# A linear-attention layer on one core: the masked scores and the state in one product of 128 rows

## The chip, the core and the metric

The kernel runs on one core of a Trainium2 chip. The core has five engines that run their own instruction streams and meet at semaphores: TensorE (PE, matrix products into the accumulation memory PSUM), VectorE (DVE), ScalarE (ACT), GpSimd (POOL) and SyncE (SP), which here only issues DMAs. The metric is the time of one execution in microseconds of device time. A single execution was also recorded by the hardware profiler; every row below is from that one.

## What is computed

Eight sequences of 1024 tokens with 512 features go through an attention layer without softmax and through a linear layer, each behind a layer norm and with a residual:

```python
def step(carry, inp):
    kv, ksum = carry
    qt, kt, vt = inp
    kv = kv + kt[..., :, None] * vt[..., None, :]
    ksum = ksum + kt
    num = jnp.einsum('bhi,bhij->bhj', qt, kv)
    den = jnp.einsum('bhi,bhi->bh', qt, ksum)[..., None] + EPS
    return ((kv, ksum), num / den)
...
q, k, v = split(x @ W_attn + b_attn); q, k = elu(q) + 1, elu(k) + 1     # 16 heads of 32
y = lax.scan(step, init, (q, k, v))[1] @ W_proj + b_proj
...
x = x + attn(layernorm(x))
x = x + ffn(layernorm(x))      # ffn: x and the weight rounded to float8, product, + bias
```

(The last lines are put together from the reference's functions.) The kernel does not step token by token: within 64 tokens it forms the scores k·q, masks them and multiplies by v; what came before the 64 tokens is held in a state of 32 x 33 numbers per head (32 columns of kv and one of ksum) that is multiplied by q.

## The kernel before

The 8192 tokens are 64 tiles of 128 (NT), four tiles are one batch of 512 columns for the projection (j, c = divmod(n, 4)), eight tiles are one sequence (PER). In a tile the first 64 tokens are half a = 0, the others a = 1.

Each engine's program is written out by hand, one loop over n with the steps of tile n in a fixed order; nothing is scheduled by a planner. On PE a tile is: `scores(n)`, `from_state(n)`, two chunks of the projection of the next batch (`ahead(chunks(n)[0])`, 12 products of 512 columns each), `k_tokens(n + 1)` (four transposes of k), the third chunk, `values(n)`, `update(n + 1)`, `proj(n - 1)` and `ffn(n - 2)`. A batch has twelve chunks, three per tile: eight of q and k features, four of v. So tiles with c = 0 and c = 1 have three feature chunks, c = 2 has two and a v chunk, c = 3 has three v chunks. I call the three chunks A, B and C. The last five tiles have one chunk or none.

- `scores(n)` makes 32 products of 32 rows x 64 columns: keys x queries of one head and half. They land in the PSUM tensor S, one bank for each of the four heads h of a group g.
- `from_state(n)` makes 16 products q x `mid` (the state after the first half, for a = 1) and 16 q x `state` (for a = 0), started into Y, the upper part of S's banks. In a sequence's first tile the 16 with `state` are left out.
- `values(n)` adds to them, in 32 products of 64 rows x 64 columns, the masked scores `sm` x `v1` (33 columns: 32 of v and a one, which gives the denominator). `valued` crosses the halves of the output, so that four such products fit side by side.
- `update(n)` makes k x v of both halves; DVE adds them up into `mid` and `state`.

A feature chunk goes from PSUM through ACT (exp L441, relu L444) and DVE (L620) into qk; a v chunk through DVE (L628) alone. The masking is split: DVE takes two of four heads (L637), ACT copies the other two out of PSUM (`scores`, into `sm`) and POOL masks them (L891). Behind `values` DVE makes the denominator, its reciprocal and y (L659 to L674), ACT and POOL split y into two halves of 16 bits, SP transposes them by DMA (`yt`), PE projects, DVE adds the result to x (L687, x1) and takes its statistics, POOL normalises (L864, L866: x2), ACT rounds x2 to float8 and copies it to bf16 (`t2`: x28, x2b), SP transposes that (`x2t`), PE makes the FFN, ACT copies it (o) and DVE adds it to x (L697).

Every engine works its instructions off in order. ACT's order in a tile was: copy of the scores, chunk A, `ln1_parts` (the upper half of xn), chunk B, `k_tokens` (ktok), `t2(n - 2)`, chunk C, yhl, o. PE's PSUM targets other than S are four banks taken in turn; a bank is free when the engine that reads it is through.

## Time and profile before

| | us |
|---|---|
| median of 3 runs | 1022.61 (1021.32 to 1024.68) |
| profiled execution, device time | 1024.16 |
| its span, first to last instruction | 1022.4 |
| PE busy | 984.3 (96%) |
| DVE busy | 687.4 (67%) |
| POOL busy | 537.7 (53%) |
| ACT busy | 457.7 (45%) |

A row of a timeline gives the start of a group of equal instructions in microseconds, how long the group lasted, engine and line, the operation, output <- input by the program's names, shapes and count. For PE the name before the comma is the moving operand and the one behind it the stationary one, whose loading is a record of its own under PEld; a product in f32 has two records of each kind. The x1 of a tile is DVE's L687, x2 POOL's L866.

### The profile page before, as it was taken

To read this page: it belongs to the slowest core of one execution; us is meant where nothing else is said; L and a number is where in the kernel's file an instruction comes from. 1 tells how busy PE (TensorE), PEld (TensorE's weight loads), DVE (VectorE), ACT (ScalarE), POOL (GpSimd) and SP (SyncE) were. 2 spreads that over 40 slices of the span, in tenths; PEclk is the share of its full clock that TensorE was granted. 3 is DMA by queue.
4 is the path that set the end of the run, shared out by engine and by line. 5 is a ranking of instruction groups with operands and counts; after the bars stand their busy time and mean duration, and the time that the engine had idled before them with its cause. 6 is when DMAs were issued, how large, how long until landed. Compare 5 with 4: busy or idle time off the path is not lost.

```text
span 1022.4 us, 43585 instructions
## 1 busy us (share of the span) xinstructions
PE 984.3 (96%) x19504; PEld 547.6 (54%) x19504; DVE 687.4 (67%) x1447; ACT 457.7 (45%) x715; POOL 537.7 (53%) x524
## 2 busy tenths in 40 slices
PE   5999999999999999999999999999999999999896
PEld 2455555555555555555555555555555555555463
DVE  6887667676667667666666666676666767655475
ACT  5653453534535354452544534354452643534322
POOL 3565575564564564564565564564464564453233
PEclk9989999999999999999999999999999999999999
DMA  8714334333434323333533345334333344322111
GB/s 271 110 34 100 70 73 85 75 80 82 77 80 88 82 70 90 80 70 88 77 82 86 75 70 91 79 70 92 71 76 94 67 83 91 64 60 54 34 57 52
DMA packets 185355, 82.51 MB, mean 81 GB/s; under 512 B 165840, under 2 KB 165840, under 8 KB 185168
## 3 DMA queue, kind: packets, MB, share of 16 engines
q1 hardware_dynamic: 185168, 79.73, 36.4%
q8 instruction: 153, 2.51, 1.0%
q14 instruction: 34, 0.28, 0.1%
HBM read 22.81 MB, written 16.78 MB: 39 GB/s over the span
## 4 chain that ended last, share of the span: by engine, by line
PE 80%; DMA 6%; DVE 4%; issue 4%; ACT 2%; SPq 1%; POOL 1%; ACTq 0%; POOLq 0%
PE R L227 64%; PE S L227 14%; DMA x2t<-x2b 6%; PE R L231 2%; DVE xnhl L614 2%; SPq L968 1%; ACT rel L444 1%; DVE raw L791 0%; DVE st L597 0%; DVE xs L687 0%; POOL st L864 0%; DVE qk L620 0%; ACT x L432 0%; DMA xs<-in_L_attn_x 0%; ACT x2b L432 0%
## 5 line engine op out<-in xcount | busy, mean ns | idle before, releaser
L227 PE MATMUL R<-xt,wh 128*128 128x512 f16 x1024 | 307.6, 383 | 2.4 <-ACT wh L432 2.4
L898 POOL TENSOR_TENSOR yhl<-y,yhl 128x512 f16<-128x512 f32 x60 | 71.4, 1190 | 328.8 <-ACT yhl L432 328.8
L620 DVE SCALAR_TENSOR_TENSOR qk<-qk,rel 128x512 f32<-128x512 f32 x128 | 124.5, 975 | 166.9 <-ACT rel L444 166.2
L227 PE MATMUL R<-xt,wl 128*128 128x512 f16 x512 | 194.4, 381 | 0.0
L227 PE MATMUL R<-wh,xt 128*128 128x512 f16 x512 | 160.3, 379 | 0.0
L864 POOL TENSOR_TENSOR st<-st,half 128x1 f32<-128x1 f32 x128 | 91.1, 711 | 129.4 <-DVE st L602 117.4
L227 PEld LDWEIGHTS R<-xt,wh 128*128 128x128 f16 x1024 | 97.1, 98 | 110.2 <-issue 4.4
L441 ACT ACTIVATE qk<-R,bqk,wm 128x512 f32<-128x512 f32 x128 | 99.5, 777 | 117.9 <-PE R L227 117.9
L227 PE MATMUL R<-wph,yt 128*128 128x512 f16 x512 | 132.9, 382 | 1.2 <-DVE yt L680 1.2
L432 ACT ACTIVATE yhl<-y 128x512 f16<-128x512 f32 x60 | 37.8, 630 | 171.9 <-DVE y L674 171.9
L886 POOL TENSOR_TENSOR xs<-xs,bp 128x512 f32<-128x512 f32 x64 | 108.8, 1705 | 0.0
L444 ACT ACTIVATE rel<-R,bqk,wm 128x512 f32<-128x512 f32 x128 | 98.4, 769 | 2.3 <-DVE qk L620 2.3
L614 DVE TENSOR_TENSOR xnhl<-xn,xnhl 128x512 f16<-128x512 f32 x56 | 85.1, 1520 | 18.0 <-ACT xnhl L432 17.9
L227 PE MATMUL R<-wl,xt 128*128 128x512 f16 x256 | 97.0, 379 | 0.0
L597 DVE BATCH_NORM_STATS2 st<-xs 128x6 f32<-128x512 f32 x128 | 88.4, 691 | 6.3 <-DMA xs<-in_L_attn_x 3.9
L628 DVE SCALAR_TENSOR_TENSOR v<-R,wm,bv 128x512 f32<-128x512 f32 x64 | 47.8, 748 | 57.9 <-PE R L227 57.8
L907 POOL TENSOR_TENSOR xs<-xs,bf 128x512 f32<-128x512 f32 x64 | 81.5, 1273 | 5.3
L227 PEld LDWEIGHTS R<-xt,wl 128*128 128x128 f16 x512 | 50.3, 98 | 61.3 <-issue 1.5
L432 ACT ACTIVATE o<-R 128x512 f16<-128x512 f32 x64 | 38.2, 597 | 100.0 <-PE R L227 100.0
L227 PEld LDWEIGHTS S<-v,sm 64*64 64x64 f32 x4096 | 65.8, 134 | 28.6 <-issue 26.7
L227 PEld LDWEIGHTS R<-wh,xt 128*128 128x128 f16 x512 | 50.0, 98 | 55.6
L891 POOL TENSOR_TENSOR sm<-sm,causal 128x512 f32<-128x512 f32 x60 | 78.9, 1315 | 0.0
(91 smaller groups left out, 1500.3 us busy)
## 6 DMA issues: line engine op xcount, KB each, us to landing
xs<-in_L_attn_x SPq DMA_DIRECT2D x64, 256.0 KB, 3.4
out<-xs SPq DMA_DIRECT2D x64, 256.0 KB, 2.6
raw<-in_L_attn_W_attn SPq DMA_DIRECT2D x3, 1024.0 KB, 9.4
xs<-in_L_attn_W_proj SPq DMA_DIRECT2D x4, 256.0 KB
raw<-in_L_ffn_weight SPq DMA_DIRECT2D x1, 1024.0 KB, 16.5
x2t<-x2b SPq DMA_TRANSPOSE x62, 3.6
xt<-xnhl SPq DMA_TRANSPOSE x60, 3.1
yt<-yhl SPq DMA_TRANSPOSE x60, 3.4
```

The source lines that it names most:

```text
L227: return e.matmul(out, a, b, start=start, stop=stop, skip_group_check=True)
L432: return e.activation(out, in_, ACT.Copy, **more)
L441: e.activation(dst[:, i, :], bank["qkv", j, i][:, :], ACT.Exp, scale=UN[i // 4], bias=bqk[:, i:i + 1])
L444: e.activation(rel[:, u % 2, :], bank["qkv", j, i][:, :], ACT.Relu, scale=UN[i // 4], bias=bqk[:, i:i + 1]).then_inc(s_relu, 1)
L597: e.bn_stats(row[:, 0:6], src).then_inc(s_bn, 1)
L614: e.tensor_tensor(xnhl[:, m % 4, 1, :], xn[:, m % 2, :], xnhl[:, m % 4, 0, :], ALU.subtract).then_inc(s_xlo, 1)
L620: e.scalar_tensor_tensor(qk[j % 2][:, i, :], qk[j % 2][:, i, :], 1.0, rel[:, (u - 1) % 2, :], ALU.min, ALU.add).then_inc(s_phi, 1)
L864: e.tensor_tensor(row[:, 10:11], row[:, 9:10], half[:, :], ALU.pow).then_inc(s_rs, 1)
L886: e.tensor_tensor(x, x, bp[:, :], ALU.add).then_inc(s_xb, 1)
L891: e.tensor_tensor(sm[:, 2:4, :, :], sm[:, 2:4, :, :], causal_over(2), ALU.mult).then_inc(s_sel, 1)
L898: e.tensor_tensor(yhl[:, n % 2, 1, :], y[:, :], yhl[:, n % 2, 0, :], ALU.subtract).then_inc(s_yl, 1)
L907: e.tensor_tensor(x, x, bf[:, :], ALU.add).then_inc(s_x1b, 1)
```

## The change

The state products are no longer products of their own. `sm`, which now lies in a part of `raw`, has for each half a all 128 partitions: on one half of them the masked scores (64 tokens), on the other the queries of two or four heads (32 features per head, two heads in 64 partitions). `v1` has 128 partitions per half as well: v of the 64 tokens on one half of them, and on the other the state of the head that is meant, with zeros where the other head of the pair stands. One product of 128 rows then gives masked scores x v plus q x state, and `values` has 32 of them, all started and ended by themselves.

- PE: `from_state` is gone. `values` has 32 products of 128 rows x 64 columns with 33 moving columns.
- ACT: the copy of scores is gone. `queries(n)` copies q into `sm` in four operations (64 partitions, 512 elements), `spread(n)` copies `state` and `mid` into `v1` in eight (32 partitions, 132 elements). `t2(n - 2)` stands at the head of the tile, ahead of `queries`.
- DVE: masks all heads in two operations of 64 partitions and 1024 elements; writes v in two of 64 partitions; makes y in one; no longer makes the lower half of xn (L614). `state` is zeroed at a sequence's start, so every tile has both states.
- POOL: no longer masks; makes the lower half of xn; at the start it clears `v1` (five slots of 1056 elements) and sets its ones.
- SP: x2t's transpose is issued ahead of xt's and of the FFN weight's.
- In tile 0 chunk C comes behind `values` and `update`, and the rounding of the FFN weight stands later.

```diff
-            def from_state(n):
...
+            def values(n):
                 src, v, j, c = parts(n)
+                pe.wait_ge(s_smd, n + 1)
+                pe.wait_ge(s_q, n + 1)
+                pe.wait_ge(s_v, n + 1)
+                pe.wait_ge(s_spread, n + 1)
                 for g in range(4):
+                    for h in range(4):
+                        for a in range(2):
+                            mm = matmul(Y[half_rows(a), h, g * W:(g + 1) * W], sm[:, h, a, g * HALF:(g + 1) * HALF],
+                                        v[:, a, 4 * g + h, :], True, True)
                 mm.then_inc(s_av, 1)
```

```diff
+            def queries(n):
...
+                if n:
+                    act.wait_ge(s_av, n)
+                for a in range(2):
+                    for p in range(2):
+                        q = src[half_rows(p), 0:4, tokens(n, a)[0]].unsqueeze(1).broadcast_to([HALF, 2, 4, HALF])
+                        dst = sm[half_rows(1 - a), 2 * p:2 * p + 2, a, :].rearrange("p h (g t) -> p h g t", g=4)
+                        made = copy(dst, q)
+                made.then_inc(s_q, 1)
+
+            def spread(n):
...
+                for a in range(2):
+                    act.wait_ge(*((s_mid, n + 1) if a else (s_state, n + 1)))
+                    held = mid if a else state[:, n % 2, :]
+                    for h in range(4):
+                        at, rows = HALF * (1 - a) + 32 * (h % 2), slice(32 * h, 32 * h + 32)
+                        made = copy(v[at:at + 32, a, :, h, :], held[rows, :].rearrange("p (g w) -> p g w", g=4))
+                made.then_inc(s_spread, 1)
...
+                    if n >= 2:
+                        t2(n - 2)
+                    if n:
+                        queries(n)
                     ahead(chunks(n)[0][:1])
+                    if n:
+                        spread(n)
```

```diff
             def scores(n):
-                for i, h in enumerate((0, 2) if tail(n) else (0,)):
...
-                    e.tensor_tensor(sm[:, h:h + 2, :, :], scored(h), causal_over(2), ALU.mult).then_inc(s_smd, 1)
+                dve.wait_ge(s_score, n + 1)
...
+                for a in range(2):
+                    dst = sm[half_rows(a), :, a, :].rearrange("p h (g t) -> p h g t", g=4)
+                    made = e.tensor_tensor(dst, scored(a), causal_over(a), ALU.mult)
+                made.then_inc(s_smd, 1)
...
             for n in range(NT + 2):
                 if 1 <= n <= NT:
                     t_y(n - 1)
+                if n >= 2:
+                    t2(n - 2)
+                if n + 8 < NT:
+                    t1(n + 8)
```

ACT, in a tile with three feature chunks (c = 0), before, the whole tile but its last row, the copy o. `qk` and `rel` are a chunk's exp and relu, `x` and `x2b` the two copies of x2:

```order
L432 ACTIVATE sm<-S 128x512
L441 ACTIVATE qk<-R,bqk,wm 128x512
L444 ACTIVATE rel<-R,bqk,wm 128x512
L432 ACTIVATE xnhl<-xn 128x512
L441 ACTIVATE qk<-R,bqk,wm 128x512
L444 ACTIVATE rel<-R,bqk,wm 128x512
L432 ACTIVATE ktok<-R 128x512
L432 ACTIVATE x<-x 128x512
L432 ACTIVATE x2b<-x 128x512
L441 ACTIVATE qk<-R,bqk,wm 128x512
L444 ACTIVATE rel<-R,bqk,wm 128x512
L432 ACTIVATE yhl<-y 128x512
```

The same engine and tile now, up to ktok; chunk C, yhl and o follow. `raw<-qk` are the query copies, `v<-state` and `v<-mid` the state copies:

```order
L407 ACTIVATE x<-x 128x512
L407 ACTIVATE x2b<-x 128x512
L407 ACTIVATE raw<-qk 64x2x256 x4
L416 ACTIVATE qk<-R,bqk,wm 128x512
L419 ACTIVATE rel<-R,bqk,wm 128x512
L407 ACTIVATE v<-state 32x4x33 x4
L407 ACTIVATE v<-mid 32x4x33 x4
L407 ACTIVATE xnhl<-xn 128x512
L416 ACTIVATE qk<-R,bqk,wm 128x512
L419 ACTIVATE rel<-R,bqk,wm 128x512
L407 ACTIVATE ktok<-R 128x512
```

The two copies of x2 moved from behind ktok to the front, and twelve new copies stand ahead of xnhl, chunk B and ktok.

PE, from one tile's values to the next one's score and state products, before:

```order
L227 MATMUL S<-v,sm 64x33 x32
L227 MATMUL R<-v,ktok 32x33 x32
L227 MATMUL R<-wph,yt 128x512 x4
L227 MATMUL R<-wpl,yt 128x512 x4
L227 MATMUL R<-wph,yt 128x512 x4
L227 MATMUL R<-wft,x2t 128x512 x4
L227 MATMUL S<-qk 64x64 x32
L227 MATMUL S<-state,qk 64x33 x4
L227 MATMUL S<-mid,qk 64x33 x4
```

and now, with the first product of the next chunk as the last row:

```order
L219 MATMUL S<-v,raw 64x33 x32
L219 MATMUL R<-v,ktok 32x33 x32
L219 MATMUL R<-wph,yt 128x512 x4
L219 MATMUL R<-wpl,yt 128x512 x4
L219 MATMUL R<-wph,yt 128x512 x4
L219 MATMUL R<-wft,x2t 128x512 x4
L219 MATMUL S<-qk 64x64 x32
L219 MATMUL R<-xt,wh 128x512 x2
```

The last two rows of before came four times in turn; they are gone, and the values read `raw` (the place of `sm`) instead of `sm`.

DVE, from the mask to x1 in a tile with c = 0, before:

```order
L637 TENSOR_TENSOR sm<-S,causal 128x512
L620 SCALAR_TENSOR_TENSOR qk<-qk,rel 128x512
L614 TENSOR_TENSOR xnhl<-xn,xnhl 128x512
L620 SCALAR_TENSOR_TENSOR qk<-qk,rel 128x512 x2
L659 TENSOR_SCALAR den<-S 128x16
L661 RECIPROCAL den<-den 128x16
L669 TENSOR_TENSOR y<-S,den 128x2x128
L674 TENSOR_TENSOR y<-S,den 64x2x128 x2
L648 TENSOR_TENSOR mid<-R,state 128x132
L651 TENSOR_TENSOR state<-R,mid 128x132
L687 SCALAR_TENSOR_TENSOR xs<-R,wm,xs 128x512
```

and now:

```order
L640 TENSOR_TENSOR raw<-S,causal 64x4x256 x2
L617 SCALAR_TENSOR_TENSOR qk<-qk,rel 128x512 x3
L665 TENSOR_SCALAR den<-S 128x16
L667 RECIPROCAL den<-den 128x16
L675 TENSOR_TENSOR y<-S,den 128x512
L651 TENSOR_TENSOR mid<-R,state 128x132
L654 TENSOR_TENSOR state<-R,mid 128x132
L686 SCALAR_TENSOR_TENSOR xs<-R,wm,xs 128x512
```

All three chunks' last steps still stand ahead of den, y and x1; xnhl is gone from this engine.

## Rows read from the trace of the kernel before

**Rows 1.** The page: busy microseconds, share of the span, instructions of each engine.

```profile
PE 984.3 (96%) x19504; PEld 547.6 (54%) x19504; DVE 687.4 (67%) x1447; ACT 457.7 (45%) x715; POOL 537.7 (53%) x524
```

**Rows 2.** PE's waits: for whom, microseconds in total, times, longest.

```profile
PE R L227 <- DMA x2t<-x2b: 5.9, 13, 0.7
```

**Rows 3.** Timeline of PE, tiles 22 to 24: start, length, instructions.

```profile
401.07 0.46 PE L227 MATMUL R<-v,ktok 64*32 64x33 f32 x32
401.46 1.04 PE L227 MATMUL R<-wph,yt 128*128 128x512 f16 x4
...
405.02 0.85 PE L227 MATMUL S<-qk 32*64 32x64 f32 x60
...
405.72 0.22 PE L227 MATMUL S<-qk 32*64 32x64 f32 x1
...
406.50 0.39 PE L227 MATMUL R<-wh,xt 128*128 128x512 f16 x1
...
414.81 1.14 PE L227 MATMUL S<-v,sm 64*64 64x33 f32 x64
415.87 0.76 PE L227 MATMUL R<-v,ktok 64*32 64x33 f32 x64
416.56 1.04 PE L227 MATMUL R<-wph,yt 128*128 128x512 f16 x4
...
420.12 0.86 PE L227 MATMUL S<-qk 32*64 32x64 f32 x61
```

**Rows 4.** PE's weight loads: by form (mean ns last), then by tile (min/median/max).

```profile
L227 PEld LDWEIGHTS S<-v,sm 64*64 64x64 f32 x4096 | 65.8, 134 | 28.6 <-issue 26.7 <-DVE sm L637 1.9
...
L227 PEld LDWEIGHTS R<-ident,wm x8: 190/190/333, 12.8 to 49.9; 128*128 128x128 f32 x8
```

**Rows 5.** Timeline of ACT, tile 24 (c = 0).

```profile
428.16 0.59 ACT L432 ACTIVATE ktok<-R 128x512 f32<-128x512 f32 x1
428.64 0.63 ACT L432 ACTIVATE x<-x 128x512 fp8e4<-128x512 f32 x1
429.30 0.63 ACT L432 ACTIVATE x2b<-x 128x512 bf16<-128x512 fp8e4 x1
429.85 0.78 ACT L441 ACTIVATE qk<-R,bqk,wm 128x512 f32<-128x512 f32 x1
430.53 0.77 ACT L444 ACTIVATE rel<-R,bqk,wm 128x512 f32<-128x512 f32 x1
```

**Rows 6.** ACT's instructions by form: a copy of 2048 elements.

```profile
L432 ACT ACTIVATE raw<-raw 128x2048 fp8e4<-128x2048 f32 x1 | 1.9, 1902 | 0.0
```

**Rows 7.** Timeline of DVE, tiles 22 to 24.

```profile
404.26 0.75 DVE L687 SCALAR_TENSOR_TENSOR xs<-R,wm,xs 128x512 f32<-128x512 f32 x1 [0.93 <-PE R L227]
...
407.80 0.68 DVE L637 TENSOR_TENSOR sm<-S,causal 128x512 f32<-128x512 f32 x1
...
431.33 0.69 DVE L620 SCALAR_TENSOR_TENSOR qk<-qk,rel 128x512 f32<-128x512 f32 x1 [1.52 <-ACT rel L444]
...
432.43 0.42 DVE L669 TENSOR_TENSOR y<-S,den 128x256 f32<-128x256 f32 x1
432.87 0.86 DVE L674 TENSOR_TENSOR y<-S,den 64x256 f32<-64x256 f32 x2
...
434.30 0.75 DVE L687 SCALAR_TENSOR_TENSOR xs<-R,wm,xs 128x512 f32<-128x512 f32 x1
```

**Rows 8.** Timeline of POOL: x2 of the tile whose x1 is above.

```profile
407.32 0.77 POOL L866 TENSOR_SCALAR x<-xs,st 128x512 f32<-128x512 f32 x1
```

**Rows 9.** Timeline of PE: first score products of tiles 1, 59, 60 and 63.

```profile
64.76 0.89 PE L227 MATMUL S<-qk 32*64 32x64 f32 x35 [2.40 <-DVE y L674]
...
955.77 0.50 PE L227 MATMUL S<-qk 32*64 32x64 f32 x33
...
970.60 0.66 PE L227 MATMUL S<-qk 32*64 32x64 f32 x37
...
999.45 0.70 PE L227 MATMUL S<-qk 32*64 32x64 f32 x40
```

More of the change, by code:

```diff
@@ L27 @@
 NR = 4
+NV = 5
 ORDER = (0, 4, 1, 5, 2, 6, 3, 7, 8, 9, 10, 11)
@@ L340, in values @@
+                mm.then_inc(s_score, 1)
             def values(n):
                 src, v, j, c = parts(n)
-                first = n % PER == 0
-                pe.wait_ge(s_smd, masked_dve(n))
-                if not tail(n):
-                    pe.wait_ge(s_sel, n + 1)
+                pe.wait_ge(s_smd, n + 1)
+                pe.wait_ge(s_q, n + 1)
                 pe.wait_ge(s_v, n + 1)
-                pe.wait_ge(s_one, 2)
-                for h in (0, 2):
-                    for g in range(4):
-                        for a, i in ((0, h), (1, h), (0, h + 1), (1, h + 1)):
-                            rows = tokens(n, a)[1]
-                            mm = matmul(Y[valued(a, i), i, g * W:(g + 1) * W], sm[rows, i, g, :],
-                                        v[rows, c, 4 * g + i, :], first and a == 0 and g == 0, True)
+                pe.wait_ge(s_spread, n + 1)
@@ L414, in _ @@
                         k_tokens(n + 1)
-                    ahead(chunks(n)[1])
+                    if n:
+                        ahead(chunks(n)[1])
                     values(n)
@@ L418, in _ @@
                         update(n + 1)
+                    if n == 0:
+                        ahead(chunks(n)[1])
                 if 1 <= n <= NT:
@@ L484, in k_tokens @@
                 copy(ktok[:, n % 2, :], bank["ktok", n][:, :]).then_inc(s_ktok, 1)
-            def scores(n):
-                if not tail(n):
-                    act.wait_ge(s_score, 4 * n + 4)
-                    if n:
-                        act.wait_ge(s_av, n)
-                    copy(sm[:, 2:4, :, :], scored(2)).then_inc(s_scopy, 1)
+            def queries(n):
+                src, v, j, c = parts(n)
+                for g in range(4):
+                    act.wait_ge(s_phi, phi_count(j, g))
+                act.wait_ge(s_wl, 6)
+                if n:
[7 more added lines that the diff above has]
+            def spread(n):
+                v = v1[:, n % NV, :, :, :].rearrange("p a (g h) w -> p a g h w", g=4)
+                act.wait_ge(s_one, 2)
+                if n >= NV:
+                    act.wait_ge(s_av, n - NV + 1)
+                for a in range(2):
[5 more added lines that the diff above has]
+                made.then_inc(s_spread, 1)
             def t2(n):
@@ L562, in _ @@
             phi(0, 7)
+            queries(0)
+            k_tokens(0)
             proj_size()
-            k_tokens(0)
             ffn_half()
@@ new lines, in v_out @@
+                dve.wait_ge(s_one, 2)
+                if n >= NV:
+                    dve.wait_ge(s_av, n - NV + 1)
+                for a in range(2):
+                    rows = half_rows(a)
+                    made = e.scalar_tensor_tensor(v1[rows, n % NV, a, :, 0:32], heads(bank["qkv", j, 8 + t][rows, :]),
+                                                  UN_V[rows], heads(bv[rows, :]), ALU.mult, ALU.add)
+                made.then_inc(s_v, 1)
+            def scores(n):
+                dve.wait_ge(s_score, n + 1)
+                dve.wait_ge(s_causal, 3)
+                if n:
+                    dve.wait_ge(s_av, n)
+                for a in range(2):
+                    dst = sm[half_rows(a), :, a, :].rearrange("p h (g t) -> p h g t", g=4)
+                    made = e.tensor_tensor(dst, scored(a), causal_over(a), ALU.mult)
+                made.then_inc(s_smd, 1)
@@ L844, in _ @@
                         t_y(n - 1)
-                    ahead(chunks(n)[1])
+                    if n:
+                        ahead(chunks(n)[1])
                     values(n)
@@ L849, in _ @@
                     if n == 0:
+                        ahead(chunks(n)[1])
                         proj_weight()
                         ffn_round()
+                    if n == 1:
+                        ffn_sum()
                 if 1 <= n <= NT:
@@ L886, in add_bp @@
                 e.tensor_tensor(x, x, bp[:, :], ALU.add).then_inc(s_xb, 1)
-            def scores(n):
-                if not tail(n):
-                    pool.wait_ge(s_scopy, n + 1)
-                    e.tensor_tensor(sm[:, 2:4, :, :], sm[:, 2:4, :, :], causal_over(2), ALU.mult).then_inc(s_sel, 1)
             def values(n):
@@ L913, in _ @@
             e.memset(half[:, :], -0.5).then_inc(s_half, 1)
-            for i in range(2):
-                e.memset(v1[i][:, :, :, 32:33], 1.0).then_inc(s_one, 1)
             for m in range(4):
@@ L926, in _ @@
             pool.wait_ge(s_causal, 3)
+            e.memset(v1[:, :, :, :, :], 0.0).then_inc(s_blank, 1)
+            pool.wait_ge(s_blank, 1)
+            for a, base, step in ((0, -HALF, 1), (1, HALF - 1, -1)):
+                ones = v1[:, :, a, :, 32:33].rearrange("p i h w -> p (i w) h")
+                e.affine_select(out=ones, in_=ones, compare_op=ALU.is_ge, fill=1.0, base=base,
+                                pattern=[[0, NV], [0, 16]], channel_multiplier=step).then_inc(s_one, 1)
             ln1(4)
```

121 lines of the change are left out of this document (40 added, 81 removed).

## The prediction

> **What bounds the kernel now.** I read the page's engine shares first, then PE's waits, then one tile's timeline engine by engine. PE is busy 96% of the span; no other engine is above 67% [rows 1]. PE's waits inside the loop are small: the largest that comes back is the one for x2t, 5.9 us in 13 places [rows 2]. So the time is the sum of PE's pieces, and these repeat. From tile 23's first score product to tile 24's is 405.02 to 420.12, 15.10 us: scores and state products 1.48 (405.02 to 406.50), three projection chunks with the k transposes 8.31 (to 414.81), values 1.06 (to 415.87), update 0.69 (to 416.56), output projection and FFN 3.56 (to 420.12) [rows 3]. The 58 full tiles 1 to 58 take 64.76 to 955.77, 891.0 us, 15.36 each; tiles 60 to 62, without chunks or with one, take 970.60 to 999.45, 28.85 us [rows 9].
>
> The other engines matter through one loop, so I note where its steps lie against a score start S. DVE's x1 (L687) starts at S - 0.76 (404.26 against 405.02) [rows 3, 7]. POOL's x2 ends at 407.32 + 0.77 = 408.09, which is S + 3.07 [rows 8]. Before, ACT copies x2 only at about S + 8.5 (428.64 against 420.12) and nobody waits long for that.
>
> **PE: what goes and what comes.** The state products go. In tile 23 the last score product starts at 405.72, 0.70 after the first; with the 0.14 that lie between the last values product (near 415.73, see below) and the update at 415.87, scores alone should last 0.84 instead of 1.48 [rows 3]. That is 0.64 less. Tiles that open a sequence (8 of 64) have half of these products; without them 56 x 0.64 = 36 us would go from PE.
>
> The values keep 32 products (64 records), but each now takes 128 rows x 64 columns, so that only two fit side by side (the column halves) where four 64 x 64 ones did. The 64 records before take 1.06 us; the last starts near 415.73 (414.81 + 1.14 - 0.22), so a step of four records takes about 0.92 / 15 = 0.06 us [rows 3]. What sets that step: a weight load of 64 columns lasts 134 ns, a load of 128 rows x 128 columns in f32 190 ns, 0.875 ns per column, so 64 columns are 0.056 us [rows 4]. The second load has 128 rows and lies on the same line, so I take it that the rows cost nothing and the columns set the step. Then 64 records in steps of two are 32 x 0.06 = 1.92, with the turnover 2.0 us: +0.94 per tile, 60 us in all. The bounds: if the step is not the load's, each record might cost what it does now, 1.06 (+0); if the two column halves do not overlap, 64 x 0.06 = 3.8 us (+2.8). I take +0.94, because the step fits the load. PE's own tile is then 15.10 - 0.64 + 0.94 = 15.4 us.
>
> On the overlap a rule can be weighed. From 401.07 to 401.46 stand 32 records of an update that reads rows 0 to 63 alone, in four column groups: 12 ns each, less than the 28 ns that 32 columns of weights take at 0.875 ns [rows 3, 4]. So loads do overlap between column groups of the same rows. The Trainium skill, "TensorE: Matmul & The Clock Gate", section "The mechanism", says that a weight load overlaps products in flight only when its row group differs; this row speaks against it. By that rule the values would take the 3.8 us, and it is a rival below.
>
> **ACT: the copies, and where they stand.** One copy of half of the heads' scores goes. Four query copies (64 partitions, 512 elements) and eight small ones of the state (32 partitions, 132 elements) come. In a row of copies ACT's next starts 0.48 after ktok (428.16 to 428.64) and 0.55 after x2b (429.30 to 429.85) [rows 5]; I take 0.53 for 512 elements. From 512 to 2048 elements a copy grows from 0.63 to 1.90 us, 0.83 ns an element [rows 5, 6], so 132 elements come at 0.53 - 0.31 = 0.22. Queries 4 x 0.53 = 2.12, state 8 x 0.22 = 1.76. No small ACT copy is in the trace: by bytes alone it would be 0.14 (state 1.1), at the price of a full copy 0.53 (4.2). I take 0.22, which keeps the fixed part of the rows, and use 0.35 as a likely upper end.
>
> ACT's work grows by 3.3 us in a tile of 15, of which it was busy 45% [rows 1], so there is room, but not where the copies are put. Its order in a tile is now: x2's two copies, queries, chunk A's exp and relu, state copies, xnhl, chunk B, ktok, chunk C, yhl, o. The first of these waits for x2 at S + 3.07, and everything stands behind it. PE wants the values at S + 0.84 + 8.31 = S + 9.15. ACT: 3.07 + 1.19 (x 0.66, x2b 0.53) + 2.12 + 1.36 (two of 0.68) + 1.76 + 0.1 = S + 9.6. That alone would cost 0.4. The rest is later still: xnhl 0.53, chunk B 1.36, ktok 0.60 end at S + 12.0, where PE (values over at 9.6 + 2.0 = 11.6) wants to update; and chunk C's relu ends at S + 13.3, behind which DVE, in order, does C's last step before it turns to y and x1.
>
> **The loop that closes.** From x1 of one tile to x1 of the next where all three chunks are features (c = 0 and 1): x1 to x2's end 3.83 [rows 7, 8]; x2's copies 1.19, queries 2.12, A 1.36, state 1.76, xnhl 0.53, B 1.36, ktok 0.53, C's exp 0.68 and relu 0.77, 0.03 [rows 5, 6]; DVE from C to y 1.10 (431.33 to 432.43), y as one operation of 512 elements 0.75 (as x1), then 0.57 through mid and state to x1 (y's end 433.73 to 434.30) [rows 7]. Sum 16.6. Where C is a v chunk (c = 2) it ends at ktok: 3.83 + 1.19 + 2.12 + 1.36 + 1.76 + 0.53 + 1.36 + 0.60 = 12.75, update 0.69, projection to x1 2.80 (401.46 to 404.26): 16.2. With no feature chunk (c = 3) it is 14.5, and PE's 15.4 decides. Of tiles 1 to 58 these are 29, 15 and 14: 481 + 244 + 216 = 940 us, +49 over 891.
>
> In the last tiles PE has 10 us of work and the loop without chunks is 3.83 + 1.19 + 2.12 + 1.86 + values 2.0 + 0.69 + 2.80 = 14.5: three of them 43.2 against 28.85, +14.3. In the last one values start at S + 8.3 instead of about 3, +5.6 with the longer product and without state products. Together +20.
>
> **What is free or nearly so.** DVE masks in two operations of 64 partitions and 1024 elements (under 2 x 1.36, twice the 0.68 of L637) from about S + 2.8 (407.80 against 405.02): over by 5.6, before 9.15 [rows 7]. v in two halves +0.75 per v, y in one -0.5, xnhl's subtraction goes to POOL where the mask of 1.3 went away: both have gaps. On SP x2's transpose now stands ahead of xt's; x2b is there at S + 4.4, xt's input later than before (behind xnhl), still some 3 us before a batch's first chunk needs it. x2t's 5.9 us of waits go, and are in my sum, which has none. POOL's clearing of v1 at the start delays layer norms that ACT and DVE reach late anyway; ACT's two microseconds for tile 0's queries lie beside PE's last chunks: 0, between -2 and +5.
>
> **Sum.** Profiled execution 1024.2 (span 1022.4, 1.8 outside it, 1.6 above the median 1022.6): 1024.2 + 49 + 20 = 1093.
>
> **Rivals.**
> 1. *PE stays the bound*: ACT's copies cost less and hide. Needed: queries and state together 2.7 instead of 3.9 us in c = 0 and 1. Then 58 x 15.4 = 894 (+3), tail +20: 1047. For it: ACT is 45% busy. Against: ten steps of the loop are measured rows. 10%.
> 2. *Faster*: the wide product costs per record what the small one did (1.06) and the copies hide too. PE's tile 14.5, 58 of them 839 (-52), tail +18: 990. It turns from slower to faster where the average tile falls under 15.0. For it: half the state work gone is real; against: the load's price per column, and that the loop does not hold a values step in c = 0 to 2 at all, so a cheap product alone saves only c = 3 and the tail (some 17 us). 5%.
> 3. *The state copies are dear* (0.35 or more): +1.04 in 44 tiles and the tail: 1143 and above. 12%.
> 4. *The column halves run one after the other*: PE's tile 17.3, 58 of them 1002 (+111), tail +27: 1162. By the rule above; the 12 ns row speaks against. 4%.
>
> My forecast with cheap to middling state copies (0.14 to 0.33: 1061 to 1135) has 67%; 2% are left for about no change. The range 1045 to 1135 takes in rival 1. Faster or slower by 0.3%, some 3 us, is about what a measurement of this kernel tells from no change: faster 5%, same 2%, slower 93%.
>
> **What would show it.** Right: PE's busy time falls or stays while its waits grow; new waits of PE for ACT's v copies before values and for ktok before update; values' 64 records in 2.0 us; tiles of 16.6, 16.6, 16.2 and 15.4 in turn; ACT waits for x2 at each tile's head; ACT's 132-element copies 0.2 apart; x2t no longer waited for. Wrong: values in 1.1 us (rival 2's half), tiles all of 15.4 (rival 1), DVE reaching x1 before PE has the projection in c = 0 and 1.

## Result and the profile after

The changed kernel takes 1200.82 us (median of 4 runs, 1196.81 to 1204.99) against 1023.64 (1021.32 to 1025.77) for the kernel before, run beside it: ratio 1.173, 95% interval 1.168 to 1.178. The sign was as forecast, the size was not: 1093 was forecast, 1135 was the upper end. The profiled execution lasts 1200.12 us, its span 1198.4; the span of before was 1022.4.

The page of the changed kernel: busy time of each engine, the granted clock in 40 slices, and the chain of work that ended last, as shares of the span (columns as in [rows 1]).

```profile
PE 1037.6 (87%) x15664; PEld 595.8 (50%) x15664; DVE 697.0 (58%) x1395; ACT 745.3 (62%) x1423; POOL 509.7 (43%) x521
...
PEclk9998999999999999999999999999999999998977
...
ACT 40%; PE 25%; DVE 14%; issue 11%; POOL 9%; DMA 0%; DVEq 0%
```

PE falls from 96% to 87%, and the chain is no longer PE's: ACT holds 40% of it, and DVE and POOL take part. It is a loop over engines, as forecast. The waits (columns as in [rows 2]) name its two joints:

```profile
ACT x L407 <- POOL x L866: 154.6, 62, 6.6
...
PE S L219 <- ACT v L407: 129.9, 62, 8.2
...
PE R L219 <- ACT ktok L407: 9.3, 22, 0.4
```

ACT waits 62 times for x2, 2.5 us each, and PE 62 times for ACT's state copies. The wait for x2t of [rows 2] is gone. By groups of instructions (busy us, mean ns of one | idle before them):

```profile
L219 PE MATMUL S<-v,raw 128*64 128x33 f32 x4096 | 154.5, 239 | 130.2 <-ACT v L407 129.9
```

One tile of ACT, tile 25 (c = 1, PE's first score product at 492.88), from the last tile's o to this tile's chunk C, answers to [rows 5]:

```profile
492.98 0.60 ACT L407 ACTIVATE o<-R 128x512 f16<-128x512 f32 x1 [1.34 <-PE R L219]
495.98 0.63 ACT L407 ACTIVATE x<-x 128x512 fp8e4<-128x512 f32 x1 [2.40 <-POOL x L866]
496.64 0.63 ACT L407 ACTIVATE x2b<-x 128x512 bf16<-128x512 fp8e4 x1
497.30 2.55 ACT L407 ACTIVATE raw<-qk 64x512 f32<-64x512 f32 x4
499.87 0.78 ACT L416 ACTIVATE qk<-R,bqk,wm 128x512 f32<-128x512 f32 x1
500.55 0.77 ACT L419 ACTIVATE rel<-R,bqk,wm 128x512 f32<-128x512 f32 x1
501.35 1.28 ACT L407 ACTIVATE v<-state 32x132 f32<-32x132 f32 x4
502.64 1.29 ACT L407 ACTIVATE v<-mid 32x132 f32<-32x132 f32 x4
503.96 0.63 ACT L407 ACTIVATE xnhl<-xn 128x512 f16<-128x512 f32 x1
...
506.96 0.79 ACT L419 ACTIVATE rel<-R,bqk,wm 128x512 f32<-128x512 f32 x1
```

POOL makes the x2 that ACT waits for:

```profile
495.18 0.77 POOL L866 TENSOR_SCALAR x<-xs,st 128x512 f32<-128x512 f32 x1
```

ACT stands idle from 493.6 to 496.0 for x2, with the queries behind it that need nothing of x2. From there it runs without a gap to chunk C's relu (507.75), and only then can DVE go on. DVE's x1 of this tile and of the next, and what stands ahead of the second (this answers to [rows 7]):

```profile
492.12 0.75 DVE L686 SCALAR_TENSOR_TENSOR xs<-R,wm,xs 128x512 f32<-128x512 f32 x1 [0.61 <-PE R L219]
...
507.78 0.69 DVE L617 SCALAR_TENSOR_TENSOR qk<-qk,rel 128x512 f32<-128x512 f32 x1 [1.14 <-ACT rel L419]
...
510.14 0.74 DVE L686 SCALAR_TENSOR_TENSOR xs<-R,wm,xs 128x512 f32<-128x512 f32 x1
```

x1 to x1 is 18.02 us (492.12 to 510.14): POOL's x2 ends at 495.95, 3.83 after x1 as forecast, ACT's unbroken run takes to 507.75, DVE the rest. PE's values in tiles 24 and 25, and the score product that opens tile 25 (answers to [rows 3]):

```profile
485.36 3.07 PE L219 MATMUL S<-v,raw 128*64 128x33 f32 x64 [1.98 <-ACT v L407]
...
492.88 0.91 PE L219 MATMUL S<-qk 32*64 32x64 f32 x64
...
504.08 2.06 PE L219 MATMUL S<-v,raw 128*64 128x33 f32 x64 [1.98 <-ACT v L407]
```

Both tiles wait 1.98 us for the state copies. In tile 25 the values take 2.06, in tile 24 the same 64 records take 3.07, at a lower clock. By stretches (length, busy PE, PEld, DVE, ACT, POOL with counts, granted clock, DMA share, GB/s): tiles 24, 25, 27 (c = 3) and 59:

```profile
474.16:492.88 18.72, 16.74 (x250) 9.90 (x249) 9.48 (x20) 12.75 (x24) 7.84 (x8) 0.91 0.27 65
492.88:510.79 17.91, 15.51 (x249) 8.81 (x248) 9.30 (x20) 12.75 (x24) 7.04 (x9) 1.00 0.30 68
...
529.73:545.69 15.96, 15.46 (x249) 8.79 (x248) 11.91 (x24) 8.62 (x18) 7.85 (x8) 1.00 0.32 76
...
1094.19:1111.66 17.47, 11.80 (x225) 7.99 (x224) 7.91 (x15) 8.09 (x17) 4.63 (x5) 0.80 0.17 40
```

So tiles last 17.9 (c = 0, 1, 2) and 16.0 (c = 3), some 18.7 to 18.9 with a stretch at the lower clock (1.2 instead of 2.4 GHz). Tiles 1 to 58 take 65.03 to 1094.19, 1029.2 us; what follows takes 104.2, before 66.6 [rows 9].

The experiments below are quoted with what was expected of each. A ratio is to the kernel before, run beside it on the same chip (its median 1021.72, 1019.5 and 1023.23 in the three larger groups of runs and 1024.45 beside the last kernel). "Head" is the place at which ACT's order of a tile begins.

### The profile page after: what moved, and what is told of

Read it like the earlier page. It is cut to its first block, busy times and chain, and to the rows that moved or that the text cites. A ratio compares the mean times of both kernels' runs of the same rounds, so it can differ in the third digit from the quotient of the medians.

```text
span 1198.4 us, 36528 instructions
## 1 busy us (share of the span) xinstructions
PE 1037.6 (87%) x15664; PEld 595.8 (50%) x15664; DVE 697.0 (58%) x1395; ACT 745.3 (62%) x1423; POOL 509.7 (43%) x521
## 4 chain that ended last, share of the span: by engine, by line
ACT 40%; PE 25%; DVE 14%; issue 11%; POOL 9%; DMA 0%; DVEq 0%
PE R L219 16%; ACT raw L407 13%; ACT v L407 10%; PE S L219 9%; ACT qk L416 5%; POOL st L864 5%; ACT rel L419 5%; POOL x L866 4%; DVE xs L686 4%; DVE st L601 4%; ACT x L407 3%; ACT x2b L407 2%; DVE st L603 1%; ACT ktok L407 1%; DVE st L606 1%
## 5 line engine op out<-in xcount | busy, mean ns | idle before, releaser
L617 DVE SCALAR_TENSOR_TENSOR qk<-qk,rel 128x512 f32<-128x512 f32 x128 | 97.3, 762 | 341.8 <-ACT rel L419 341.6
L219 PE MATMUL S<-v,raw 128*64 128x33 f32 x4096 | 154.5, 239 | 130.2 <-ACT v L407 129.9
L219 PEld LDWEIGHTS S<-v,raw 128*64 128x64 f32 x4096 | 148.6, 157 | 158.4 <-issue 157.6
L881 POOL TENSOR_TENSOR xnhl<-xn,xnhl 128x512 f16<-128x512 f32 x60 | 72.4, 1207 | 230.1 <-ACT xnhl L407 230.1
L407 ACT ACTIVATE raw<-qk 64x512 f32<-64x512 f32 x256 | 160.9, 628 | 3.8
L640 DVE TENSOR_TENSOR raw<-S,causal 64x1024 f32<-64x1024 f32 x128 | 155.7, 1217 | 0.9
L219 PE MATMUL R<-wph,yt 128*128 128x512 f16 x512 | 141.6, 402 | 1.4 <-DVE yt L679 1.4
L407 ACT ACTIVATE x<-x 128x512 fp8e4<-128x512 f32 x62 | 39.1, 630 | 154.6 <-POOL x L866 154.6
L629 DVE SCALAR_TENSOR_TENSOR v<-R,wm,bv 64x512 f32<-64x512 f32 x128 | 96.0, 750 | 16.4 <-PE R L219 13.9
L888 POOL TENSOR_TENSOR xs<-xs,bp 128x512 f32<-128x512 f32 x64 | 82.4, 1288 | 4.7
```

Of the source, the lines that this page charges most:

```text
L219: return e.matmul(out, a, b, start=start, stop=stop, skip_group_check=True)
L407: return e.activation(out, in_, ACT.Copy, **more)
L617: e.scalar_tensor_tensor(qk[j % 2][:, i, :], qk[j % 2][:, i, :], 1.0, rel[:, (u - 1) % 2, :], ALU.min, ALU.add).then_inc(s_phi, 1)
L629: made = e.scalar_tensor_tensor(v1[rows, n % NV, a, :, 0:32], heads(bank["qkv", j, 8 + t][rows, :]), UN_V[rows], heads(bv[rows, :]), ALU.m ...
L640: made = e.tensor_tensor(dst, scored(a), causal_over(a), ALU.mult)
L881: e.tensor_tensor(xnhl[:, m % 4, 1, :], xn[:, m % 2, :], xnhl[:, m % 4, 0, :], ALU.subtract).then_inc(s_xlo, 1)
```

## Experiment 1: the product without its copies

```diff
             def queries(n):
...
+                if n:
+                    return
...
             def spread(n):
...
+                if n >= NV:
+                    return
```

PE's waits for these copies, and DVE's, are lifted as well. The kernel so leaves the state's part out of y from tile 5 on.

> The changed kernel without its query copies after tile 0 and without its state copies after tile 4, so the state's part of y is left out from then on; the wide products and all else stay. Theory A (the loop through ACT's twelve copies behind x2 carries the loss): PE is the bound again with tiles of 15.4 us, 58 of them 894, and the last tiles near the kernel before: 1035 to 1055. Theory B (the wide product and the changed work of PE carry it): little changes, 1150 or more. Theory C (half of it each, the copies and the place of x2's copies): 1080 to 1120.

Measured: 1034.10 us (1033.37 to 1035.59), ratio 1.012 (1.011 to 1.014). PE, one values product between the scores of two tiles:

```profile
483.67 0.91 PE L219 MATMUL S<-qk 32*64 32x64 f32 x64
492.82 2.06 PE L219 MATMUL S<-v,raw 128*64 128x33 f32 x64
499.06 0.91 PE L219 MATMUL S<-qk 32*64 32x64 f32 x64
```

Tiles of 15.39 (483.67 to 499.06) without a wait. So PE's own tile is the 15.4 that was forecast, and the product costs what was worked out; what is left up to 1201, some 167 us, comes in with the copies.

## Experiment 2: x2's copies back behind ktok, and the head alone in the kernel before

In the changed kernel:

```diff
-                    if n >= 2:
-                        t2(n - 2)
                     if n:
                         queries(n)
...
                         k_tokens(n + 1)
+                    if n >= 2:
+                        t2(n - 2)
```

> The changed kernel with x2's two copies back behind ktok on ACT, all copies kept. Theory A1 (it is the wait for x2 at the head, with the copies queued behind it, not ACT's amount of work, 12.8 us of 17.9 busy in a tile): queries start at S + 0.7 instead of S + 4.4, values find their copies, tiles of 15.4 to 15.8: 1040 to 1070, and the clock stays at full. Theory A2 (twelve copies are too much for ACT wherever they stand): above 1120.

Measured: 1051.31 us (1046.74 to 1052.63), ratio 1.028 (1.026 to 1.030): 149 us under the changed kernel, with every copy still there. Most tiles are 15.39; PE waits 10.8 us in 14 places for x2t again.

In the kernel before, the opposite edit, with the transposes' order on SP:

```diff
                 if n < NT:
+                    if n >= 2:
+                        t2(n - 2)
                     scores(n)
...
-                if 2 <= n < NT:
-                    t2(n - 2)
...
+                if n >= 2:
+                    t2(n - 2)
                 if n + 8 < NT:
                     t1(n + 8)
-                if n >= 2:
-                    t2(n - 2)
```

> The kernel before with x2's two copies at the tile's head on ACT and x2t's transpose ahead of xt's on SP, nothing else of the change. Theory: ACT waits for x2 as in the changed kernel, but only the copy of the scores (0.6 us) and no twelve copies stand between it and chunk A; the loop is 3.83 + 1.2 + 0.6 + 1.4 + 0.5 + 1.4 + 0.5 + 1.45 and 3 on DVE = 13.9, under PE's 15.1. The 13 waits for x2t and the stretched tiles (some 10 us in all) go: 1010 to 1020. Rival: the place at the head costs by itself: above 1035.

Measured: 1014.00 us (1013.17 to 1016.22), ratio 0.993 (0.991 to 0.994), below both kernels. ACT at a tile's head, and the chain:

```profile
416.50 0.63 ACT L432 ACTIVATE x<-x 128x512 fp8e4<-128x512 f32 x1 [2.40 <-POOL x L866]
```

```profile
PE 93%; DVE 2%; POOL 1%; issue 1%; ACT 1%; DMA 0%; ACTq 0%; POOLq 0%
```

ACT waits for x2 exactly as long as in the changed kernel (2.40), and here it costs nothing, since the loop behind it is short. No x2t wait is left, and tiles 1 to 58 take 874.6 us instead of 891.0, nearly all 15.1 or less. The place of x2's copies is therefore harmless alone, and so nearly are the other copies alone (experiment 2, first part): it is the two together that cost some 150 us.

A third place, t2 behind chunk A and the layer norm's part, with SP's order as in b_x2_head:

> The kernel before with x2's two copies behind the first chunk and xnhl on ACT, where x2 has long been made, and x2t's transpose ahead of xt's on SP. If the gain of the version with the copies at the head comes from x2t landing before PE asks for it, this one is the same: tiles of 15.10, 1010 to 1018. If it were from the place at the head itself: like the kernel before, 1018 to 1024.

Measured: 1014.58 us (1010.69 to 1016.57), ratio 0.991 (0.988 to 0.995), the same as at the head. The gain of b_x2_head is x2t landing in time, not the head. How much of it is SP's order and how much the earlier copies was not taken apart; in a_x2_back SP's new order alone left PE 10.8 us of waits for x2t.

## Experiment 3: two lines swapped

```diff
-                    if n >= 2:
-                        t2(n - 2)
                     if n:
                         queries(n)
+                    if n >= 2:
+                        t2(n - 2)
```

> The changed kernel with two lines of ACT's tile swapped: the four query copies ahead of x2's two copies. No work is added or left out. Theory A (the loop from x1 through POOL's x2 and ACT): 2.6 us leave the loop, since the queries then run while x2 is still being made; 17.9 - 2.6 = 15.3, so PE's 15.4 decides in nearly every tile, and the last tiles shorten as well: 1030 to 1055. Rival (ACT's whole row of work decides, 12.8 us busy and its waits): above 1120.

Measured: 1052.46 us (1050.19 to 1052.76), ratio 1.028 (1.025 to 1.031). Same instructions, 148 us less. ACT at the head:

```profile
470.07 2.55 ACT L407 ACTIVATE raw<-qk 64x512 f32<-64x512 f32 x4
472.64 0.63 ACT L407 ACTIVATE x<-x 128x512 fp8e4<-128x512 f32 x1
```

The queries fill the time in which x2 is on its way, and ACT then waits for x2 4.3 us in the whole run (154.6 in the changed kernel). The tiles come back to PE's 15.4: with the 2.6 us of queries out of it the loop is under that, and PE sets the pace. That gives 2.5 us in each of 42 tiles and 0.6 in each of the 14 with c = 3, some 114 us; the rest comes in tile 2 (20.1 instead of 23.5), behind tile 58 (88.8 us instead of 104.2) and from the clock, which rises to 0.988 from 0.953. PE's waits for v fall to 24.1 us in 6 places.

## Experiment 4: fewer copies in the loop

The four copies of mid left out:

```diff
-                for a in range(2):
+                for a in range(2 if n < NV else 1):
```

> The changed kernel without the four copies of the state after the first half (mid) from tile 5 on, which leaves that part out of y. A dose of the suspected cost: 1.3 us out of ACT's row. Theory A: every tile with c = 0 to 2 gets 1.3 us shorter plus the clock's share (0.8 in a third of them), c = 3 0.57, the last tiles 1.3 to 2.5 each: 60 to 90 us faster than the changed kernel, 1110 to 1140. If the copies are only partly on the path: under 40 us.

Measured: 1119.27 us (1117.66 to 1120.03), ratio 1.097 (1.094 to 1.101). Most tiles are 16.61 to 16.71 for c = 0 to 2 and 15.39 for c = 3. PE's score products of two tiles in turn, 16.62 apart:

```profile
448.52 0.91 PE L219 MATMUL S<-qk 32*64 32x64 f32 x64
...
465.14 0.91 PE L219 MATMUL S<-qk 32*64 32x64 f32 x64
```

The four copies took 1.29 us (502.64, above), and the tiles gave 1.2 to 1.3 (17.92 - 16.71, 17.92 - 16.61): what stands in ACT's run counts one for one, or nearly. That is the loop, shown by its slope.

## Experiment 5: what the clock took

The lower clock follows PE's waits, so this kernel shortens them without touching the loop: six products of chunk C are made twice, ahead of it.

```diff
+                for a, b in mms[:again]:
+                    matmul(out[:, :], a, b, True, True)
...
-                        ahead(chunks(n)[1])
+                        ahead(chunks(n)[1], 6 if c < 3 and n > 1 else 0)
```

> The changed kernel with six redundant products (1.3 us) ahead of chunk C in tiles with c = 0 to 2, so that PE is busy in a part of the time in which it waits for the state copies; the result is the same. Theory (17 of the stretches at half clock inside the loop make values and the first projection products 0.8 to 1.0 us longer in their tile, and follow from PE's 2 us waits): these go, the clock rises from 0.953, 10 to 18 us faster than the changed kernel, 1183 to 1191. Rival (the clock is hidden in the waits): no change, or slower by up to 44 x 0.3.

Measured: 1184.42 us (1184.03 to 1185.5), ratio 1.160 (1.158 to 1.161): with 1.3 us more of work in 43 tiles it is 16 us faster than the changed kernel. A tile as a stretch:

```profile
467.19:485.11 17.92, 16.77 (x255) 9.41 (x255) 9.30 (x20) 12.75 (x24) 7.05 (x8) 1.00 0.29 68
```

PE's wait for the state copies is down from 1.98 to some 0.5 to 0.7 us a tile. The tile is the loop's 17.92 again, and in the steady tiles the granted clock stays at the higher level (2.4 GHz); over the run it is 0.983 instead of 0.953. So some 16 us of the loss are stretches at 1.2 GHz, and they followed waits of 2 us of an engine that was otherwise busy.

## Experiment 6: what a copy costs on ACT

The copies in a row were forecast 0.53 (512 elements) and 0.22 (132) apart and came 0.64 and 0.325 apart. Series of copies that nobody waits for, behind the last tile of the kernel before, tell why. First, all of them beginning at partition 0:

```diff
+            for i in range(4):
+                copy(raw[:, 0, i, :], y[:, :])
+            for i in range(4):
+                copy(raw[0:HALF, 2, i, :], y[0:HALF, :])
+            for i in range(4):
+                copy(qk[0][:, 4 + i, 0:4 * W], y[:, 0:4 * W])
+            for i in range(4):
+                copy(qk[0][0:32, 4 + i, 256:256 + 4 * W], y[0:32, 0:4 * W])
...
```

> The kernel before with eight series of four independent ACT copies behind its last instruction, each series of another form: how far apart do they start? 128 x 512 and 64 x 512 from SBUF, 128 x 132 and 32 x 132 from SBUF, 128 x 512 and 64 x 512 from PSUM, 128 x 512 with the queries' pattern. Theory P (a copy from SBUF behind one from SBUF never starts before the other's end; the 0.1 us of overlap in the rows of before all have PSUM on one side): 128 x 512 from SBUF 0.64 apart, from PSUM 0.5. Theory Q (copies of fewer than 128 partitions don't overlap): 128 x 512 0.53 apart, 64 x 512 0.64.

Measured (one execution, 1028.29 us), four plus four copies of 512 elements, then four plus four of 132 (a row names the shape of its first copy: the second four of each have 64 and 32 partitions), and four with the queries' pattern:

```profile
1014.56 4.25 ACT L432 ACTIVATE raw<-y 128x512 f32<-128x512 f32 x8
1018.72 1.71 ACT L432 ACTIVATE qk<-y 128x132 f32<-128x132 f32 x8
...
1024.16 2.17 ACT L432 ACTIVATE xt<-qk 128x512 f32<-128x512 f32 x4
```

Eight in 4.16 us (1014.56 to 1018.72), 0.52 apart, with 128 partitions and with 64 alike; eight small ones in 1.62, 0.20 apart, with 32 partitions as with 128; the queries' pattern four in 2.17, the last one 0.63 long, 0.51 apart. Both theories fell, for neither the number of partitions nor the queries' pattern costs anything. What was left is where a copy's partitions lie against those of the one ahead:

```diff
+            for i in range(4):
+                copy(raw[up, 0, i, :], y[low, :])
...
+            for i in range(4):
+                at = up if i % 2 else low
+                copy(raw[at, 2, i, :], y[at, :])
+            for i in range(4):
+                copy(qk[0][32:64, i, 0:4 * W], y[0:32, 0:4 * W])
+            for i in range(4):
+                copy(qk[0][0:32, i, 0:4 * W], y[32 * i:32 * i + 32, 0:4 * W])
+            for i in range(4):
+                copy(qk[0][32 * i:32 * i + 32, 4, 0:4 * W], y[0:32, 0:4 * W])
...
```

> The kernel before with eight series of four ACT copies behind its last instruction. In the series before, copies with all partitions from 0 on started 0.52 (512 elements) and 0.20 (132) apart; in the changed kernel they started 0.64 and 0.325 apart. Theory S (a copy waits for the end of the one before when the set of partitions changes between them): only the series that alternate the half or the quarter of source or target are 0.64 or 0.32 apart. Theory T (when source and target lie on different partitions): the series with a constant shift are slow as well. Theory U (targets with gaps in them): only the last two series, with the patterns of the queries and of the state, are slow.

Measured (one execution, 1032.02 us), each row a stretch of the series: from the lower to the upper half each time; alternating halves (two of them); 32 partitions, from the first to the second group of 32 each time; alternating sources (with the last copy of the series ahead); all three kinds in order of time:

```profile
1016.60 2.19 ACT L432 ACTIVATE raw<-y 64x512 f32<-64x512 f32 x4
...
1020.99 1.27 ACT L432 ACTIVATE raw<-y 64x512 f32<-64x512 f32 x2
...
1023.54 0.92 ACT L432 ACTIVATE qk<-y 32x132 f32<-32x132 f32 x4
1024.17 1.59 ACT L432 ACTIVATE qk<-y 32x132 f32<-32x132 f32 x5
```

Four in 2.19, the last one 0.63 long, are 0.52 apart; two in 1.27 are 0.64 apart; four in 0.92, the last 0.31 long, 0.20; five in 1.59, 0.32. Whether source or target moves makes no difference, and a constant shift between them costs nothing. So in these series ACT's next copy starts some 0.11 us before the end of the one ahead only when it reads and writes the same partitions as that one. (That it does is not enough for every pair: x2b, which reads what x has just written, starts 0.03 us after x's end, 496.64 against 496.61.) The queries read alternating halves, and the state copies go to and from changing groups of 32: every one of them starts after the end of the one before. The Trainium skill, "ScalarE: Activation LUTs", section "What ACT_TABLE_LOAD costs", says that ACTIVATEs in a row overlap by about 93 ns; the rows with a constant place come near it (0.11), those with a changing place show no overlap, and here the measurement decides.

## Experiment 7: the state copies on DVE

```diff
-                        made = copy(v[at:at + 32, a, :, h, :], held[rows, :].rearrange("p (g w) -> p g w", g=4))
+                        made = e.tensor_copy(v[at:at + 32, a, :, h, :], held[rows, :].rearrange("p (g w) -> p g w", g=4))
...
                     scores(n)
+                    spread(n)
```

ACT's own `spread` and its two calls are gone.

> The changed kernel with the eight state copies on DVE, behind the mask, instead of on ACT; x2's copies stay at the head. Theory A: 2.6 us leave the loop of ACT; DVE makes them in some 2 us from S + 5.3, before values at S + 9.15. Loop of c = 0 and 1: 17.9 - 2.6 = 15.3, PE's 15.4 decides: 1040 to 1065 with the last tiles. Rival (ACT's loop is held by the x2 wait and the queries alone): above 1100.

Measured: 1082.45 us (1080.27 to 1084.8), ratio 1.062 (1.058 to 1.065). Tiles of 15.39 for c = 0 to 2, as the shorter run on ACT wants, but 17.07 for c = 3, so the 1040 to 1065 that was expected was missed by 17 us. In tile 27 (c = 3) PE waits 0.56 us for DVE's state copies and 0.99 for the DVE that has a v chunk's bank to empty behind them: the work moved to a second engine that others wait for. With x2's copies behind ktok besides (both edits together):

> The changed kernel with the state copies on DVE and x2's copies back behind ktok. If PE is the bound in every tile, this is its floor: 58 x 15.4 = 894 and last tiles like before, 1025 to 1045: the wide product's price of +0.3 us per tile is left, so it is not faster than the kernel before. Rival: faster than before (under 1018), if PE's steps get shorter when nobody waits.

Measured: 1103.31 us (1101.07 to 1105.16), ratio 1.082 (1.079 to 1.085). This missed as well (1025 to 1045 was expected): the two cures together are worse than either. Most tiles are 15.92, and 16.97 for c = 3. DVE's state copies as a group (mean 773 ns), then DVE's copies in one tile, then POOL in the same stretch:

```profile
L637 DVE COPY v<-state 32x132 f32<-32x132 f32 x256 | 197.9, 773 | 4.6
```

```profile
493.05 0.63 DVE L637 COPY v<-state 32x132 f32<-32x132 f32 x1
493.70 1.35 DVE L637 COPY v<-state 32x132 f32<-32x132 f32 x1
495.06 1.10 DVE L637 COPY v<-state 32x132 f32<-32x132 f32 x1
...
496.41 0.92 DVE L637 COPY v<-mid 32x132 f32<-32x132 f32 x4
```

```profile
492.83 0.77 POOL L864 TENSOR_SCALAR xn<-xs,st 128x512 f32<-128x512 f32 x1
493.69 1.27 POOL L886 TENSOR_TENSOR xs<-xs,bp 128x512 f32<-128x512 f32 x1
494.92 1.15 POOL L879 TENSOR_TENSOR xnhl<-xn,xnhl 128x512 f16<-128x512 f32 x1
```

The first three state copies end at 493.68, 495.05 and 496.16, each 0.08 or 0.09 after the end of a POOL operation (493.60, 494.96, 496.07); the four of mid, with POOL idle, take 0.92 together. In a_spread_dve, where DVE's copies stand otherwise against POOL's work, the eight cost less: state 568 ns and mid 281 in the mean, against 773 and 223. To tell a block from mere lateness, one more kernel writes the same copies as another kind of DVE operation:

```diff
-                        made = e.tensor_copy(v[at:at + 32, a, :, h, :], held[rows, :].rearrange("p (g w) -> p g w", g=4))
+                        src = held[rows, :].rearrange("p (g w) -> p g w", g=4)
+                        made = e.tensor_reduce(v[at:at + 32, a, :, h, :], src.unsqueeze(3), AX.X, ALU.add)
```

> a_both with one thing changed: the eight state copies on DVE are written as reductions over a last axis of one element, the same numbers to the same places. In a_both a copy takes 0.22 us when POOL is idle, and when one meets a POOL operation it ends 0.09 us after that operation (ends 493.68, 495.05, 496.16 against POOL's 493.60, 494.96, 496.07); the state copies last 773 ns in the mean. Theory L (lock): DVE's copy and POOL's operations exclude each other, and a DVE operation of another kind does not. Then a reduction takes 0.2 to 0.3 us whatever POOL does, the tiles come to PE's 15.4 in all four positions, and the time falls from 1103 by 44 x 0.5 + 14 x 1.6 + some 5 in the last tiles to about 1055 (1045 to 1065). The Trainium skill, SBUF - State Buffer, section Who interferes with whom, states this exclusion for DVE copies and excepts the reduction. Theory D (DVE is merely late: the copies wait for something else, or POOL's traffic slows any DVE operation on these rows): the reductions last 0.6 us and more beside POOL as well, tiles stay 15.9 and 17.0, 1095 to 1110.

Measured: 1047.27 us (1045.83 to 1047.94), ratio 1.021 (1.017 to 1.025), 56 us under a_both. DVE's state copies as a group, then four of them in one tile, then the POOL operation beside them:

```profile
L638 DVE TENSOR_REDUCE v<-state 32x132 f32<-32x132 f32 x256 | 72.5, 283 | 4.7
```

```profile
490.67 1.17 DVE L638 TENSOR_REDUCE v<-state 32x132 f32<-32x132 f32 x4
```

```profile
491.31 1.27 POOL L887 TENSOR_TENSOR xs<-xs,bp 128x512 f32<-128x512 f32 x1
```

The reductions take 0.28 us beside POOL's operation (state 283 ns in the mean, mid 280), a little more than a free copy (0.22), and tiles are 15.39 again. So the copies were blocked by POOL's operations. This is what the Trainium skill, "SBUF — State Buffer", section "Who interferes with whom", says: a DVE copy can run in a mode that uses two port pairs, the second of which is shared with GpSimd, whoever issues first holds it for the whole instruction, and a reduction never takes part. The trace agrees, copy by copy, for DVE behind POOL; that POOL waits for a DVE copy is not shown by these rows.

## Why the direction was right and the size wrong

What held, by the prediction's own steps:

- *PE's pieces.* Values 2.06 us as recorded, 1.99 from their start to the update's in a_no_copies (2.0 forecast), scores 0.84 (0.84), PE's tile 15.39 (15.4). The step by columns of weights came out, and with it that the two column halves overlap: rivals 2 and 4 fell on one row, `S<-v,raw` at 504.08. Over b_x2_head, where nothing waits either, the change without its copies costs 1034.1 - 1014.0 = 20 us.
- *The loop and its joints.* ACT waits for x2 at the head, PE for v, now and then for ktok; in tile 25 DVE reaches x1 with the projection done (tile 24, whose values ran at the lower clock, has DVE wait 0.61 for it at 492.12); x1 to x2's end 3.83 to the digit. Rival 1 (PE stays the bound) fell on PE's 129.9 us of waits.
- *What was held to be free.* The mask on DVE, the subtraction on POOL and SP's order cost nothing in steady tiles, and x2t's waits went: a_no_copies has all of this and tiles of 15.39.

**The step that failed** is the price of a copy in the ACT part: "I take 0.53 for 512 elements", from the rows ktok to x and x2b to qk [rows 5], and from it 0.22 for 132. Those rows keep the same 128 partitions, and the copies to be priced do not (experiment 6). Measured in tile 25 against the forecast: x and x2b to the first query 1.32 instead of 1.19, queries 2.57 instead of 2.12, relu to the first state copy 0.80 instead of 0.68, state 2.61 instead of 1.76. That is 1.55 a loop, and by experiment 4 what is added there counts one for one or nearly. Added to the forecast's 16.6 and 16.2 it gives 18.1 and 17.8, where the tiles are 17.92; with no chunk in it, the loop of 14.5 becomes 15.9, where c = 3 has 15.96. Rival 3 looked at the right place, but its state copies of 0.35 or more did not come (0.325 apart), and its 1.04 us a tile left out the queries. The range ended at 1135 because it gave a margin to the state copies alone: none to the queries, the clock, the opening or the last tiles.

The miss of 107 us (1200.1 - 1093) adds up as follows. Tiles 1 to 58 took 1029.2 instead of 940, 89 more:

- 56 of them, tiles 3 to 58, at the loop's 17.92 (42 tiles) and 15.96 (14 tiles) are 976.1; the forecast had 28 x 16.6 + 14 x 16.2 + 14 x 15.4 = 907.2. **The copies' price: 69 us.** In it are 8 us of c = 3, where the forecast let PE decide and the loop of 15.96 is 0.57 above PE's 15.39.
- Measured, the 56 took 990.6 (103.63 to 1094.19): **14 us more, the clock.** The forecast had no term for it. Experiment 5 gives 16 for the whole kernel.
- **Tile 2, 23.5 instead of 16.2: 7 us,** less 1.5 that tile 1 came under. This was not foreseen either. DVE and PE of the changed kernel there:

```profile
80.50 3.45 DVE L790 TENSOR_TENSOR raw<-raw 128x512 bf16<-128x512 fp8e4 x4
83.88 0.74 DVE L686 SCALAR_TENSOR_TENSOR xs<-R,wm,xs 128x512 f32<-128x512 f32 x1
...
95.43 3.63 PE L219 MATMUL S<-v,raw 128*64 128x33 f32 x64 [6.10 <-ACT v L407]
```

The reordered opening puts a weight sum of 3.45 us on DVE right ahead of the first x1, which so starts 3.8 us after tile 2's first score product (80.11); before it was 0.5 (82.70 against 82.19). Through x2 and ACT's head, behind which the state copies stand, PE gets it: it waits 6.10 us instead of 1.98, and its values then take 3.63, at the lower clock. Some 1.7 of the 7 us are the copies' price once more. The prediction had looked at POOL's clearing and ACT's queries in the opening, not at this.

Behind tile 58 the time was 104.2 instead of 66.6 + 20: 18 more. Tiles 60 to 62 took 1111.66 to 1165.16, 17.8 each instead of 14.4. Copies account for 1.4 of it; most of the rest is of the kind that tile 59 shows, PE of the changed kernel:

```profile
1103.91 3.58 PE L219 MATMUL S<-v,raw 128*64 128x33 f32 x64 [5.67 <-ACT v L407]
```

After a wait of 5.67 us the values take 3.58 instead of 2.06, at the lower clock; in tiles 60 to 62 the same step takes 3.3 to 3.6. Tile 59 itself was 17.5 instead of the 14.8 that I had left as it was (2.6), the last tile 4.7 over. Together 89 + 18 is the 107. In the prediction's own sums, three loops of 14.49 are 43.5 where it has 43.2, and 58 x 14.5 is 841 where rival 2 has 839; nothing hangs on either.

In sum the way from before to after, in single steps that were run: x2's copies moved for themselves -8 (b_x2_head 1014.0), the product +20 (a_no_copies 1034.1), its copies ahead of x2's +18 (a_q_first 1052.5; 16 of them behind tile 58), and x2's copies ahead of the queries +148 (1200.8). By way of a_x2_back (1051.3) the last step is the same move on ACT as the first: it is worth -8 with a short loop behind it and +149 with the long one.

What stays open: the state copies on POOL were not tried. Nor was a_both_reduce with x2's copies right behind the queries, so the best form of the changed product found here, 1047.3, need not be the lowest; no form of it came under the kernel before, and b_x2_head, without the product, did.

## What to carry to other kernels

An engine works in order, so a copy that needs nothing belongs ahead of one that waits for a late result: two lines swapped were worth 148 us of 1201. Before new work goes on a half idle engine, follow the loop that each iteration closes (here x1, POOL, ACT, DVE, x1) and see whether it stays under the bound engine's time, for below that it is nearly free and above it each microsecond counts in full. A price taken from neighbouring rows holds only for rows that share what the new instruction has, its partitions too.

## What the runs showed of the hardware

- In series of independent copies ACT overlaps one with the one ahead by 0.11 us at unchanged partitions and not at changed ones: 512 elements 0.52 against 0.64 apart, 132 elements 0.20 against 0.32.
- A DVE copy of 32x132 in f32 takes 0.22 us, and took 0.63 to 1.35 where it met POOL operations; the same as a reduction takes 0.28 beside them.
- Products of 128 rows with 64 columns of f32 weights go two side by side, 0.06 us per pair (64 records in 1.99 us); those of 64 rows went four side by side, 0.06 us per four (1.06). The step was the same for twice the rows.
- In tile 24 PE was busy for 16.74 of 18.72 us and waited 1.98 in one place, and what followed the wait ran in part at the lower level (granted clock 0.91 over the tile); tile 25, with the same wait, stayed at the higher one (1.00). Over the run it was 0.953 against 0.994 before, and filling part of those waits with useless products made the kernel 16 us faster.
